# Index copies and inverse roots moved off GpSimd in the two edge stages of a graph network

## The reference

```python
# layer 0, message passing: attention weights per edge, rows of h gathered by src, summed by dst
e = leaky_relu(a_src[src] + a_dst[dst], 0.2)
out = segment_sum(h[src] * softmax_by_dst(e)[:, :, None], dst)
# layer 1, message passing: rows of y gathered by src, products with an edge network, summed by dst
h = silu(edge_scalars @ fc_w1 / sqrt(8)) * 1.679
w = h @ fc_w2 / 8
mids = products(w, y[edge_src], edge_attr)
agg = segment_sum(mids, edge_dst)
# layer 1, attention part: keys and values normalized per head of 64, then a head-wise Gram matrix
k = (k - mean(k)) * rsqrt(var(k) + 1e-5);  v = (v - mean(v)) * rsqrt(var(v) + 1e-5)
dots = einsum('bhnd,bhne->bhde', k, v)
```

## Time and profile before

| | before |
|---|---|
| median of three runs | 3345.35 us |
| the profiled execution | 3341.32 us |
| its span, first to last instruction | 3339.6 us |
| mean granted TensorE clock | 0.917 |

### The profile page before, as it was taken

One profiled execution on the slowest core, in us unless ns is written; L12 is line 12 of the kernel. 1 busy time (PEld: TensorE's weight loads), 2 busy tenths in 40 slices (PEclk: granted clock), 3 DMA queues, 4 the chain that ended last, 5 costly groups with the idle time before them and its releaser, 6 DMA issues. The chain is left out here.

```text
span 3339.6 us, 78237 instructions
## 1 busy us (share of the span) xinstructions
PE 2808.7 (84%) x21943; PEld 2141.9 (64%) x21943; DVE 2282.9 (68%) x6620; ACT 1311.4 (39%) x4384; POOL 1983.1 (59%) x2317
## 2 busy tenths in 40 slices
PE   6677777777777788699997899999999999889399
PEld 4566666666666666588884455555555555568387
DVE  5577777777777777476665677777777777768522
ACT  5333333333333246333332344444444444248122
POOL 3577777777777711011114787787787877722254
PEclk9788888888888899899997899999999999999599
DMA  6544444444444457422223333333333333437221
GB/s 190 164 112 110 111 114 111 112 110 111 114 110 114 127 148 197 139 80 87 82 83 105 103 108 106 107 107 106 107 106 106 107 106 106 120 112 203 58 52 47
DMA packets 239081, 375.71 MB, mean 113 GB/s; under 512 B 88190, under 2 KB 145606, under 8 KB 238762
## 3 DMA queue, kind: packets, MB, share of 16 engines
q0 software_dynamic: 89712, 230.26, 25.1%
q1 hardware_dynamic: 147482, 140.83, 15.0%
q10 hardware_dynamic: 1696, 2.62, 0.2%
HBM read 310.75 MB, written 62.84 MB: 112 GB/s over the span
## 5 line engine op out<-in xcount | busy, mean ns | idle before, releaser
L596 POOL DMA_INDIRECT e_rows<-tab,e_ix x830 | 790.1, 952 | 234.6 <-issue 203.0
L2029 POOL DMA_INDIRECT e_rows<-tab,e_ix x828 | 792.3, 957 | 227.5 <-issue 202.6
L1020 PE MATMUL e_pU<-e_ohp,e_rows 128*128 128x128 f32 x3340 | 518.8, 323 | 5.0 <-DVE e_ohp L868 4.9
L1020 PEld LDWEIGHTS e_pU<-e_ohp,e_rows 128*128 128x128 f32 x3340 | 483.4, 232 | 23.8 <-issue 6.8
L2195 DVE TENSOR_TENSOR e_msg<-e_pW,e_rows 128x384 f32<-128x384 f32 x834 | 422.1, 548 | 0.0
L2259 PE MATMUL e_pU<-e_msg,e_oh 128*32 128x128 f32 (+1 forms) x6672 | 371.7, 310 | 11.3 <-DVE sum L2155 11.0
L2245 PE MATMUL e_pW<-e_w,e_hT 64*128 64x256 f32 x1668 | 317.2, 431 | 43.2 <-DVE e_msg L2195 37.6
L2193 DVE TENSOR_TENSOR e_msg<-e_pW,e_rows 128x256 f32<-128x256 f32 x417 | 175.5, 421 | 250.1 <-PE e_pW L2245 200.7
L705 ACT COPY e_ohT<-e_pT 64x640 bf16<-64x640 bf16 x167 | 114.6, 686 | 546.7 <-PE e_pT L1001 516.5
L2259 PEld LDWEIGHTS e_pU<-e_msg,e_oh 128*32 128x32 f32 x6672 | 243.1, 112 | 132.3 <-issue 71.9
L1001 PE MATMUL e_pT<-e_identB,e_oh 128*64 128x128 bf16 x835 | 86.3, 242 | 248.2 <-DVE e_oh L494 224.3
(11 more groups left out here) (458 smaller groups left out, 5394.8 us busy)
## 6 DMA issues: line engine op xcount, KB each, us to landing
e_rows<-tab,e_ix POOLq DMA_INDIRECT x1658
xnT<-f_xnT SPq DMA_DIRECT2D x25, 250.0 KB, 3.0
e_xk<-xnT SPq DMA_DIRECT2D x25, 250.0 KB
xnT<-b_xT SPq DMA_DIRECT2D x25, 250.0 KB, 2.9
m_xnT<-xnT SPq DMA_DIRECT2D x25, 250.0 KB
xnT<-m_xT SPq DMA_DIRECT2D x25, 250.0 KB, 2.6
ffn_norm<-xnT SPq DMA_DIRECT2D x25, 250.0 KB
tab<-f_hrow SPq DMA_DIRECT2D x25, 227.5 KB
```

What stands on the lines that cost most here:

```text
L596: nc.gpsimd.indirect_dma_start(out=rows[:, s, j, :], out_offset=None, in_=env["tab0"], in_offset=bass.IndirectOffsetOnAxis(ap=at[:, j:j + ...
L1020: nc.tensor.matmul(pU[:, s % 2, 2 * W * k:2 * W * (k + 1)], rows[:, s, j, 128 * k:128 * k + 128], ohp[:, s % 3, j, 2 * k:2 * k + 2, :], st ...
L2029: nc.gpsimd.indirect_dma_start(out=rows[:, r % PER, j, :], out_offset=None, in_=env["tab1"], in_offset=bass.IndirectOffsetOnAxis(ap=at[:, ...
```

## The change

Three edits. In both edge stages GpSimd's stream keeps only the gathers: the copies into `ix` go to ScalarE, which does them 6 groups ahead in `edges0` (behind the exponential p, in front of pp) and 10 groups ahead in `edges1` (behind `copied`, in front of `silu`); `ix` grows to 6 and 10 buffers. Groups outside the hardware loop gather by `srcI` itself. In `edges1` the power on GpSimd goes; ScalarE takes a square root (`root`, at the end of its steps with q = 3 and 0) and VectorE a reciprocal (`inverse`, at the end of its steps with q = 3 and 0). In `ffn0` ScalarE's wait for `s_lin` moves from ahead of the first gelu to ahead of the first use in `rows`.

```diff
@@ edges0
-        ix = sb("ix", [P, 2, GT], I32)
+        ix = sb("ix", [P, SLOTS, GT], I32)
@@ edges0, GpSimd
-                        at = ix[:, s % 2, :] if lo >= 1 else srcI[:, 0:GT]
-                        if lo >= 1:
-                            pool.wait_ge(s_ix, g)
+                        at = ix[:, s, :] if k is not None else srcI[:, g * GT:g * GT + GT]
+                        if k is not None:
+                            pool.wait_ge(s_ix, g - SLOTS + 1)
...
-                            if j == 3 and hi <= GROUPS - 2:
-                                nc.gpsimd.tensor_copy(ix[:, (s + 1) % 2, :], srcI[:, bass.ds((g + 1) * GT, GT)])\
-                                  .then_inc(s_ix, 1)
@@ edges0, ScalarE
                         nc.scalar.activation(p[:, s % 3, :, :], ee[:, 4 + s % 2, :, :], ACT.Exp)
+                        if hi < LATE:
+                            nc.scalar.copy(ix[:, s, :], srcI[:, bass.ds((g + SLOTS) * GT, GT)]).then_inc(s_ix, 1)
@@ ffn0, ScalarE
                 act.wait_ge(s_b1, 32)
-                act.wait_ge(s_lin, 96)
...
                     hold(act, s_Y, u + 1)
+                    if lo == 0:
+                        act.wait_ge(s_lin, 96)
@@ edges1, GpSimd
-                    def inverse_roots(c, t):
-                        hold(pool, s_ab, 2 * c + t + 1)
-                        nc.gpsimd.tensor_tensor(out=ri[:, t, :], in0=ab[:, t, :], in1=mhalf, op=ALU.pow).then_inc(s_ri, 1)
-
                     def step(g, r, lo, hi, c):
-                        at = ix[:, r % 2, :] if lo >= 1 else srcI[:, 0:T1]
-                        if lo >= 1:
-                            pool.wait_ge(s_ix, g)
+                        at = ix[:, r, :] if lo < hi else srcI[:, g * T1:g * T1 + T1]
+                        if lo < hi:
+                            pool.wait_ge(s_ix, g - 2 * PER + 1)
...
-                            if j == 3 and hi <= GROUPS1 - 2:
-                                nc.gpsimd.tensor_copy(ix[:, (r + 1) % 2, :], srcI[:, bass.ds((g + 1) * T1, T1)])\
-                                  .then_inc(s_ix, 1)
...
-                            if j == 1 and behind_chunk(lo) and r % PER in (2, 4):
-                                inverse_roots(c - 1, r % PER // 2 - 1)
@@ edges1, ScalarE
+                    def root(c, t):
+                        hold(act, s_ab, 2 * c + t + 1)
+                        nc.scalar.activation(sd[:, t, :], ab[:, t, :], ACT.Sqrt).then_inc(s_sd, 1)
+
...
                             copied(g - 1, lo - 1)
+                        if lo >= 1 and hi <= LAST:
+                            nc.scalar.copy(ix[:, (r - 1) % (2 * PER), :], srcI[:, bass.ds((g + 2 * PER - 1) * T1, T1)])\
+                              .then_inc(s_ix, 1)
                         if hi <= GROUPS1 - 2:
                             silu(g + 1, r + 1, lo + 1)
+                        if behind_chunk(lo) and q == 0:
+                            root(c - 1, 1)
+                        if in_chunks(hi) and q == 3:
+                            root(c, 0)
@@ edges1, VectorE
+                    def inverse(c, t):
+                        v.wait_ge(s_sd, 2 * c + t + 1)
+                        nc.vector.reciprocal(ri[:, t, :], sd[:, t, :]).then_inc(s_ri, 1)
...
                         if in_chunks(hi) and q in (2, 4):
                             variances(c, q // 2 - 1)
+                        if in_chunks(hi) and q == 3:
+                            inverse(c, 0)
+                        if behind_chunk(lo) and q == 0:
+                            inverse(c - 1, 1)
```

More of the change, by code:

```diff
@@ L1960, in edges1 @@
         pb = lambda n, s: ctx.enter_context(nc.psum_tensor("e1_" + n, s, F32))
-        ix = sb("ix", [P, 2, T1], I32)
+        ix = sb("ix", [P, 2 * PER, T1], I32)
         rows = sb("rows", [P, PER, T1, C])
@@ L1974, in edges1 @@
         small = env["pself"][:, :, :].rearrange("p t h -> p (t h)")
-        ssk, ssv, ab, _, ri = (small[:, TILES + 16 * i:TILES + 16 * i + 16].rearrange("p (t h) -> p t h", t=2) for i in range(5))
-        mhalf = small[:, TILES + 88:TILES + 96]
+        ssk, ssv, ab, sd, ri = (small[:, TILES + 16 * i:TILES + 16 * i + 16].rearrange("p (t h) -> p t h", t=2) for i in range(5))
         ta = small[:, TILES + 80:TILES + 88]
@@ L1991, in edges1 @@
                                      "added"))
-        s_wk, s_xk, s_kv, s_read, s_ab, s_ri, s_vs, s_gram, s_cp = (
-            sem("k1_" + n) for n in ("weights", "x", "products", "read", "squares", "scales", "scaled",
+        s_wk, s_xk, s_kv, s_read, s_ab, s_sd, s_ri, s_vs, s_gram, s_cp = (
+            sem("k1_" + n) for n in ("weights", "x", "products", "read", "squares", "deviations", "scales", "scaled",
                                      "gram", "kept"))
@@ L2032, in step @@
                               .then_inc(s_row[j], 16)
-                            if j == 1 and behind_chunk(lo) and r % PER in (2, 4):
-                                inverse_roots(c - 1, r % PER // 2 - 1)
-                    nc.gpsimd.memset(mhalf, -0.5)
-                    pool.drain()
                     turns(pool, step)
@@ L2353, in edges1 @@
                     s_es + [s_ix, s_T, s_esT, s_F, s_h, s_W, s_msg, s_eq, s_oh, s_acc, s_us, s_flip, s_add,
-                            s_wk, s_xk, s_kv, s_read, s_ab, s_ri, s_vs, s_gram, s_cp, s_wf, s_dT, s_M, s_m1, s_G, s_wl],
+                            s_wk, s_xk, s_kv, s_read, s_ab, s_sd, s_ri, s_vs, s_gram, s_cp, s_wf, s_dT, s_M, s_m1, s_G, s_wl],
                     W1, SLOTS1 * SUB)
```

## The result

The kernel now takes 3264.98 us, median of 4 runs (3260.37 to 3272.18), beside 3345.59 for the kernel before in the same comparison (4 runs, 3344.71 to 3346.80). The ratio is 0.9761, with a 95% interval of 0.9742 to 0.9780, so it is faster by 74 to 86 us. The profiled execution took 3267.07 us with a span of 3265.3; the span before was 3339.6, so 74.3 us are to be found between the two traces. That is 6.3 us less than the 80.6 between the medians, because the profiled execution of the kernel before lies 4.3 us under that kernel's median here, and the one after 2.1 us above its own.

A forecast was written before the change was run, and what follows sets the result against it. GpSimd was taken to pace both edge stages, with TensorE next in `edges1`. Gains of 15 + 6.6 + 62.7 = 84.3 us take the profiled 3341.3 to 3257 us, 3261 against the median; forecast 3250 to 3278, range 3240 to 3300.

The forecast's parts named there:

- part 1: `edges0`: index copies leave GpSimd, 0.09 us for each of 156 groups plus small waits, 15 us gained (bounds 0 and 31).
- part 3: `edges1`: copies and powers leave GpSimd, TensorE's steps then bound most of a chunk at 39.5 us; 62.7 us gained by step 138.
- part 2: `ffn0`: moved wait removes TensorE's 3.82 us pause and 2.8 us of slow clock behind it; 6.6 us gained.
- I add 0.3 us: `edges1`: allowance per chunk for TensorE's low clock after short pauses, on steps summing to 39.2 us.
- The tail: Last 13 steps of `edges1`, to step 138: 94 us at 7.23 each, 5 for closing products, 2 for low clock.
- the closing products: Last 13 steps of `edges1`: products TensorE does in one piece, put at 5 us.
- GpSimd's whole time: Rival, `edges1`: all of GpSimd's time, 91 us, comes back as TensorE's steps shrink as well; 3233 us, chance 0.05.
- GpSimd is not late until then: `edges1`: step 5 starts at 1838.28 as before, since GpSimd delays nothing earlier.
- ScalarE's new work: `edges1`: roots with two table changes each, and `inverse` on VectorE, costed at 0 (bounds 0 and 0.4 us per chunk).
- The clock in every chunk: Rival, `edges1`: TensorE's clock falls in all 24 chunks, about 1.2 us each, 29 us more; 3290 us, chance 0.10.
- Late load: Rival, `edges1`: table load back delays hT, TensorE misses 1.2 us in q = 4, 0.7 in q = 1; 3309 us, chance 0.06.
- the uncovered root: Rival, `edges1`: the root's new chain is not covered, 3.1 us for each of 50 roots; 3415 us, slower, chance 0.05.

The follow-up runs named there:

- kernel a: Kernel before with only the index copies of `edges0` moved from GpSimd to ScalarE; 3324.41 us beside 3342.65, ratio 0.9948.
- b: Kernel before with only the `s_lin` wait of `ffn0` moved; 3332.32 us beside 3342.65, ratio 0.9974.
- g: Changed kernel plus a Silu and a Sqrt of one element ahead of the load back, q = 4 and 1; 4287.02 us beside a kernel before of 4240.76.

## Why the prediction was right, and where it was not

**The sum.** Predicted 84.3 us, measured 80.6 between the medians, 74.3 between the two profiled spans. The sum was worked out on the profiled execution, so 74.3 is the like number, 10 us short; that the medians come within 4 us is in part luck. By the trace the 10 us are 2.4 in part 1, 7.3 in part 3 (62.7 predicted, 55.4 measured from step 5 to 138: 3.9 in the chunks, 3.4 behind them), and 1.0 in stretches for which I had nothing, less 0.6 that part 2 and the way into `edges1` gave more.

**Part 1** was mis-sized: 15 predicted, 12.6 in the trace. GpSimd itself did what the sum says. Its first 156 groups take 981.8 us after and 995.8 before, 13.9 less, and 14.7 less in kernel a, so a copy cost 0.09 us. What I had at nothing is the stretch behind them. The last eleven groups, which I counted as neutral, give 0.5 us back (1.4 in kernel a), and from the last gather to the start of `ffn0` it is 203.1 us after and 201.8 before (203.2 in kernel a). What makes those two stretches longer when the gathers end sooner stays open. VectorE's waits for rows went from 103 times and 85.8 us to 98 times and 69.2, so GpSimd is still the pace there.

**Part 2** held: 6.6 predicted, 7.1 measured in the changed kernel and in b. The first gelu comes 8.6 us sooner against its stage's start, with some 9 predicted.

**Part 3, what becomes the bound,** held. The steps were predicted at 8.40, 7.45, 6.84, 9.04 and 7.45 from q = 2; their means over the stage are 8.33, 7.44, 6.87, 9.56 and 7.44. The term that was mis-sized is the clock's: "I add 0.3 us". Twelve of 24 steps with q = 0 have a fall and take 10.08 - 9.07 = 1.0 us more, so the falls cost 0.50 us a chunk, 12 us in the stage in place of 7. Without them a chunk would be 39.66 - 0.50 = 39.16, and I had 39.2. All of it is in q = 0, behind the pause of 1.08 us that ends q = 4; I had named that pause and taken its price too low. The tail is the same error: 101 us predicted, 104.4 measured, where four steps of 8.82 us stand among those of 7.23 (6.4 us more), each with a mean clock of 0.81, and I had 2 us for it. Against that the closing products added 3.5 us and not 5.

**Part 3, why the time was lost before,** was incomplete. My sum went from step to step of the kernel before (1838.28 and 2949.95) and so contained the first chunk's stall without my having seen it; I had even written that 23 windows repeat one picture and not asked for the 24th. "GpSimd is not late until then" was right only up to step 5. The gain came out nearly right all the same, because the sum ran between two measured points and not over the waits that it named. Of the 54.5 us of the chunks, 13.8 have no cause in my account, and that the edit takes them away was luck, not insight. The rival that gave GpSimd's whole time back (91 us) left that stall out and would have come out too small had it been true.

**ScalarE's new work** cost nothing that the trace shows. Timeline of ScalarE after, root in q = 3, load back and silu in q = 4:

```profile
2283.90 1.28 ACT L2095 ACT_TABLE_LOAD   x1
2285.20 0.21 ACT L2095 ACTIVATE pself<-pself 125x8 f32<-125x8 f32 x1
...
2290.82 1.28 ACT L2071 ACT_TABLE_LOAD   x1 [0.15 <-PE e_pH L2238]
2292.12 0.49 ACT L2071 ACTIVATE e_hT<-e_pH 128x384 f32<-128x384 f32 x1
```

hT ends at 2292.12 + 0.49 = 2292.61 and TensorE takes it at 2292.74: the load fits by 0.13 us, as predicted by 0.12. Nor are the 1.08 us in q = 4 a wait for hT: they were there before, when hT ended at 2386.31 + 0.49 = 2386.80 and TensorE came at 2388.20. VectorE's 50 reciprocals have 0.1 us of idle time before them in all.

None of the stage's 101 table loads has over 0.02 us of idle time behind it, and the root's load starts 0.02 us behind silu. The rule of the Trainium skill, "ScalarE: Activation LUTs", "What ACT_TABLE_LOAD costs", that a change of set also drains for 1380 ns is not borne out here: silu starts 0.02 us behind its load, as in the earlier trace rows, and q = 4 kept its 6.87 us. Whether a load costs more where nothing covers it was what g should have shown, and it stays open.

**The rivals.** GpSimd's whole time (3233) fell, for GpSimd waits for buffers 36.6 us. The clock in every chunk (3290) was half true: 12 of 24 chunks have it, at 1.0 us each and not 1.2. Late load (3309) and the uncovered root (3415) fell by the rows above.

## What to carry to other kernels

When the pacing engine is relieved, read the steps of the next one by one and look for the short pauses left in them: while GpSimd paced `edges1`, a fall of TensorE's clock was absorbed, and afterwards it was paid in full, 1.0 us each. A short pause next to a full step asks for work to be moved into it; that brought some 34 us more here, and the clock stayed at 1.00. And where an in-order engine produces a small result between long rows of its own work, ask how far ahead it must be for its consumer: the price isn't its duration but a stall at the start of the loop.

## What the runs showed of the hardware that I had not expected

A fall of the granted clock cost nothing while GpSimd was the pace: in the kernel before a chunk with a fall took 42.9 us and the next 39.7, 82.6 for the two, like any other pair (2 x 41.41). The executions of the kernel before spread over 2 us in the first comparison and over 11 (3336.11 to 3346.89) in the second.

The same kernel on the same chip took 4241 us and, an hour later, 3342. In the traces of the kernels built on the changed one the difference lies in the two stages with indirect gathers, where in stretches TensorE's instructions come 0.7 us apart without a visible wait.

GpSimd's indirect gathers have a beat inside a group, 0.95 us and 0.30 between, in every kernel looked at and in either condition. A copy of 0.20 us between two of them costs 0.08 to 0.09: the idle time behind the copy is 0.16 in place of 0.30 (gather to 1798.88, copy 0.19, next gather at 1799.24 in the kernel before).
